# A graph layer on one core: the late nodes' x part of the hidden layer moved from the end of the program to its start

## What is computed

```python
agg = jax.ops.segment_sum(edge_attr, col, num_segments=x.shape[0])
h = jnp.concatenate([x, agg, u[batch]], axis=1)
h = jax.nn.relu(h @ W1 + b1)
out = h @ W2 + b2
return out + x
...
x = _layernorm(x + _L0_gnn_ref(x, edge_index, edge_attr_128, ...), axis=-1)
```

## Time and profile before

| | us |
|---|---|
| median of 3 runs | 185.27 (185.25 to 185.79) |
| the profiled execution | 185.73 |
| its span, first to last instruction | 184.0 |

### The profile page before, as it was taken

One profiled execution on the slowest core, in us unless ns is written; L12 is line 12 of the kernel. 1 busy time (PEld: TensorE's weight loads), 2 busy tenths in 40 slices (PEclk: granted clock), 3 DMA queues, 4 the chain that ended last, 5 costly groups with the idle time before them and its releaser, 6 DMA issues.

```text
span 184.0 us, 5378 instructions
## 1 busy us (share of the span) xinstructions
PE 154.1 (84%) x2195; PEld 113.9 (62%) x2195; DVE 115.4 (63%) x369; ACT 51.5 (28%) x110; POOL 25.4 (14%) x29
## 2 busy tenths in 40 slices
PE   0056979979979979969979999899889799899970
PEld 0046855955955956845846858467458568677850
DVE  6847499568376385485495466954933745877371
ACT  2021233223323313313313343133133241233230
POOL 7800030110200200200200204002003230000000
PEclk9999999999999999999999999999999999999997
DMA  5999999999999999999999999999999999998011
GB/s 119 315 352 373 374 375 373 371 373 374 374 374 373 375 372 373 376 372 373 374 373 374 375 373 374 375 373 360 363 374 374 371 374 370 367 398 303 11 43 33
DMA packets 42196, 62.07 MB, mean 337 GB/s; under 512 B 1975, under 2 KB 39541, under 8 KB 42170
## 3 DMA queue, kind: packets, MB, share of 16 engines
q1 hardware_dynamic: 41046, 61.23, 95.0%
q10 hardware_dynamic: 1124, 0.48, 1.2%
HBM read 58.50 MB, written 3.20 MB: 335 GB/s over the span
## 4 chain that ended last, share of the span: by engine, by line
PE 44%; DMA 39%; SPq 8%; DVE 4%; ACT 1%; issue 1%; DVEq 0%
DMA edge_ring<-in_edge_attr_dram 37%; PE sum_ps L845 17%; PE turn_ps L867 7%; PE hid_ps L907 6%; PE hid_ps L900 6%; PE out_ps L920 5%; SPq L276 4%; SPq L291 3%; DMA base_row<-in_dst_dram 2%; DVE bases L568 2%; PE xt_ps L920 1%; PE xt_ps L882 1%; DVE local_rows L576 1%; ACT local_t L429 1%; PE xt_ps L834 1%
## 5 line engine op out<-in xcount | busy, mean ns | idle before, releaser
L845 PE MATMUL sum_ps<-edge_ring,onehot 128*32 128x128 f32 x1662 | 58.5, 284 | 13.0 <-DMA edge_ring<-in_edge_attr_dram 10.8
L845 PEld LDWEIGHTS sum_ps<-edge_ring,onehot 128*32 128x32 f32 x1662 | 45.2, 113 | 27.9 <-DMA edge_ring<-in_edge_attr_dram 13.3
L630 DVE TENSOR_TENSOR agg_t<-agg_t,turn_ps 128x128 f32 x70 | 20.2, 288 | 56.7 <-PE turn_ps L867 52.6
L594 DVE TENSOR_TENSOR onehot<-iota,local_t 128x768 f32<-128x768 f32 (+1 forms) x40 | 33.6, 843 | 3.0 <-ACT local_t L429 2.4
L402 POOL TENSOR_TENSOR x_all<-x_all,half_b 128x512 f32<-128x512 f32 (+3 forms) x16 | 17.7, 1115 | 127.4 <-PE xt_ps L882 127.4
L466 ACT ACTIVATE hid_t<-hid_ps,bias 128x512 f32<-128x512 f32 (+3 forms) x32 | 18.1, 584 | 37.1 <-PE hid_ps L907 37.1
L867 PE MATMUL turn_ps<-place,sums 128*128 128x128 f32 (+1 forms) x140 | 26.5, 306 | 0.0
L907 PE MATMUL hid_ps<-agg_t,w_a 128*128 128x512 f32 (+3 forms) x64 | 24.1, 500 | 0.6 <-DVE agg_t L630 0.5
L867 PEld LDWEIGHTS turn_ps<-place,sums 128*128 128x128 f32 (+1 forms) x140 | 18.9, 192 | 8.0 <-issue 7.9
L920 PE MATMUL out_ps<-w_sb,hid_t 128*128 128x128 f32 (+1 forms) x176 | 21.9, 275 | 0.0
L441 ACT COPY sums<-sum_ps 128x256 f32<-128x256 f32 (+2 forms) x40 | 13.6, 341 | 25.9 <-PE sum_ps L845 25.9
(11 more groups left out here) (64 smaller groups left out, 73.0 us busy)
## 6 DMA issues: line engine op xcount, KB each, us to landing
edge_ring<-in_edge_attr_dram SPq DMA_DIRECT2D x69, 768.0 KB, 12.1
x_all<-in_x_dram SPq DMA_DIRECT2D x10, 256.0 KB, 10.5
out_dram<-x_all SPq DMA_DIRECT2D x1, 2304.0 KB
dst_rows<-in_dst_dram SPq DMA_DIRECT2D x1, 384.0 KB
x_all<-in_x_dram SPq DMA_DIRECT2D x1, 384.0 KB, 11.1
out_dram<-x_all SPq DMA_DIRECT2D x3, 128.0 KB
out_dram<-x_all SPq DMA_DIRECT2D x1, 256.0 KB
w_x<-in_L_gnn_W_dram ACTq DMA_DIRECT2D x1, 128.0 KB, 5.9
```

The source lines that it names most:

```text
L594: nc.vector.tensor_tensor(onehot[0:ROWS, b % BUFFERS, 0:k * TILES], cols, loc, ALU.is_equal).then_inc(onehot_ready, 1)
L630: nc.vector.tensor_tensor(to, to, turn_ps[b % 2][:, i * SPAN:(i + 1) * SPAN], ALU.add).then_inc(group_added, 1)
L845: last = nc.tensor.matmul(bank[c * WIN:(c + 1) * WIN], onehot[0:p, b % BUFFERS, i * TILES + c * R + r], edge_ring[0:p, slot, c * R + r], s ...
```

## The change

**Start.** The late x is loaded behind the destinations and ahead of group 0, which now stands behind the wait for the pad. `w1_x` is ACT's first load. PE turns the late x in three parts into banks of PSUM that are free at that time, ACT copies them (`copy_x_late`), PE multiplies them by `w1_x` (`sum_x_late`), and ACT keeps the products in SBUF, in `x_hid_late` (`keep_x_hidden`). The first part's product stands ahead of the turning of the destinations, the other two behind it, and PE starts the first batch when all are kept. x of blocks 7, 8 and 9 is loaded two groups earlier than before.

**Late pieces.** `sum_hidden_a` of a late piece starts its own PSUM group. DVE adds the kept product to it into `x_hid_late` (`add_x_hidden`, one add for each half of the hidden layer), and ACT's relu reads from there.

**Order.** The hand-written lists from step 30 on are replaced by loops on `out_step` and `hidden_step`, with `hidden_step` of A set to 31. On DVE `normalize` stands ahead of `step` there, and `add_x_hidden` behind `moments`. ACT takes the root ahead of the copy of the step. The limits for the check of the input's form are made with 15 operations and one reduction in place of 10 and 9.

```diff
@@ -27,6 +27,7 @@
 J = BLOCK // P
 EPS = 1e-5
 GEN_TILES = 10
+COMPLETE_AT = [6, 12, 18, 24, 30, 36, 40, 46, 52, 58, 60, 63, 66, 67, 69]
...
@@ -84,15 +87,25 @@
         return range(batch_first[b], batch_first[b + 1])
 
 
-    hidden_step = [batch_first.index(complete_at[n]) for n in range(n_big)]
+    late_step = batch_first.index(single0)
+    hidden_step = [batch_first.index(complete_at[n]) for n in range(n_pieces)]
+    hidden_step[A] = max(hidden_step[A], late_step + 1)
     out_step = [b + 1 for b in hidden_step]
     turn_x_step = [1] + out_step[:n_big - 1]
-
-
-
-    x_parts = [(n,) for n in range(n_big)] + [(A, B), (C_, D, E), (REST,)]
-    x_load_at = {1: 0} | {IT * n: n for n in range(1, n_big)}
-    x_late_at = 53
...
+
+
+    late_parts = [(A, B), (C_, D, E), (REST,)]
+    n_late = len(late_parts)
+    x_parts = late_parts + [(n,) for n in range(n_big)]
+    x_load_at = {1: 0} | {complete_at[n - 1]: n for n in range(1, n_big)}
+    x_order = [n for part in x_parts for n in part]
+    late_cols = [sum(pieces[n][1] * pieces[n][2] for n in part) for part in late_parts]
+    late_col = [sum(late_cols[:k]) for k in range(n_late)]
...
+        late_turned = [turn_ps[0], turn_ps[1], sum_ps[0]]
+        late_hidden = [[sum_ps[1][:, :], hid_ps[1][:, :]], [turn_ps[0][:, :], turn_ps[1][:, :]],
+                       [sum_ps[0][:, m * late_cols[2]:(m + 1) * late_cols[2]] for m in range(m_chunks)]]
...
-            load_group(0)
+                                 ).then_inc(x_landed[2], 16)
+
 
             sp.wait_ge(pad_set, 1)
-            sp.dma_start(dst_rows[64:full_grp], dst_full[64:full_grp]).then_inc(dst_landed, 16)
-            sp.dma_start(dst_rows[full_grp:n_grp, 0, 0:rest_edges],
+            sp.dma_start(dst_rows[pad0:full_grp], dst_full[pad0:full_grp]).then_inc(dst_landed, 16)
+            sp.dma_start(dst_rows[full_grp:n_grp].rearrange("g c e -> g (c e)")[:, 0:rest_edges],
                          dst[full_grp * EDGES_GRP:n_edges].rearrange("(o e) -> o e", o=1)).then_inc(dst_landed, 16)
-            for g in range(1, n_grp):
+            load_x_late()
+            for g in range(n_grp):
                 load_group(g)
                 if g in x_load_at:
                     load_x(x_load_at[g])
-                if g == x_late_at:
-                    load_x_late()
...
+            act.dma_start(w1_x[:], w1[0:d, :]).then_inc(w1_x_landed, 16)
             act.dma_start(base_row[0:1, 0:n_grp],
                           dst.rearrange("(o e) -> o e", o=1)[:, 0:n_edges:EDGES_GRP],
                           allow_slow_non_contiguous=True).then_inc(bases_landed, 16)
             for to, src in loads:
                 act.dma_start(to, src, allow_slow_non_contiguous=True).then_inc(weights_landed, 16)
+
+            def copy_x_late(k):
+                act.wait_ge(x_turned, k + 1)
+                at = 0
+                for n in late_parts[k]:
+                    _, p, j = pieces[n]
+                    last = nc.scalar.copy(x_t_late[:, late_cols_of(n)].rearrange("f (p j) -> f j p", j=j),
+                                          late_turned[k][:, at:at + p * j].rearrange("f (j p) -> f j p", j=j))
+                    at += p * j
+                last.then_inc(x_t_ready, 1)
+
+            def keep_x_hidden(k):
+                act.wait_ge(late_x_summed, k + 1)
+                for m in range(m_chunks):
+                    last = nc.scalar.copy(x_hid_late[:, m, late_col[k]:late_col[k] + late_cols[k]], late_hidden[k][m])
+                last.then_inc(late_x_ready, 1)
+
+            for k in range(n_late):
+                copy_x_late(k)
+            keep_x_hidden(0)
 
             lt = local_t[:].rearrange("p (g t) -> p t g", t=TILES)
             t0 = 0
@@ -430,6 +482,8 @@
                                       ps[0:ROWS, 0:(t1 - t0) * n_grp].rearrange("p (t g) -> p t g", g=n_grp))
...
+                nc.scalar.copy(x_t[:, n % 2].rearrange("f (p j) -> f j p", j=J),
+                               xt_ps[:, :].rearrange("f (j p) -> f j p", j=J)).then_inc(x_t_ready, 1)
 
             def relu(n):
                 _, p, j = pieces[n]
+                late = n >= n_big
                 for m in range(m_chunks):
-
-                    act.wait_ge(hidden_summed, m_chunks * n + (m + 1 if n < n_big else m_chunks))
+                    if late:
...
+                    else:
+                        act.wait_ge(hidden_summed, m_chunks * n + m + 1)
                     if n >= 2 and m == 0:
 
                         act.wait_ge(out_summed, n - 1)
+                    src = x_hid_late[:, m, late_cols_of(n)] if late else hidden_bank(n, m)
...
                                                        rstd_n[:, jj:jj + 1], ALU.subtract, ALU.mult)
                     last.then_inc(normalized, 1)
 
+            def add_x_hidden(n):
+
+                dve.wait_ge(hidden_summed, m_chunks * (n + 1))
+                if n == A:
+                    dve.wait_ge(late_x_ready, n_late)
+                for m in range(m_chunks):
+                    xh = x_hid_late[:, m, late_cols_of(n)]
+                    nc.vector.tensor_tensor(xh, hidden_bank(n, m), xh, ALU.add).then_inc(late_added, 1)
+
             def moments(n):
...
-            late_step = batch_first.index(single0)
             for b in range(late_step):
                 step(b)
                 if CHECK0 <= b < CHECK0 + 3:
                     check(b - CHECK0)
-                for n in range(n_big):
+                for n in range(LAST):
                     if out_step[n] + 1 == b:
                         moments(n)
                     if out_step[n] + 2 == b:
                         normalize(n)
-            b = late_step
-            step(b)
-            step(b + 1)
-            moments(LAST)
-            step(b + 2)
-            normalize(LAST)
-            step(b + 3)
-            moments(A)
-            step(b + 4)
-            normalize(A)
-            step(b + 5)
-            moments(B)
-            step(b + 6)
-            normalize(B)
-            step(b + 7)
-            step(b + 8)
-            moments(C_)
-            step(b + 9)
-            normalize(C_)
+            for b in range(late_step, n_batch):
+                for n in range(LAST, n_pieces):
+                    if out_step[n] + 2 == b:
+                        normalize(n)
+                step(b)
+                for n in range(LAST, n_pieces):
+                    if out_step[n] + 1 == b:
+                        moments(n)
+                for n in range(A, E):
+                    if hidden_step[n] == b:
+                        add_x_hidden(n)
             add_batch(n_batch - 1)
-            moments(D)
-            normalize(D)
+            add_x_hidden(E)
+            add_x_hidden(REST)
+            for n in range(LAST, E):
+                if out_step[n] + 1 >= n_batch:
+                    moments(n)
+                if out_step[n] + 2 >= n_batch:
+                    normalize(n)
...
+            def turn_x_late(k):
+                pe.wait_ge(x_landed[k], 32 if k == n_late - 1 else 16)
+                if k == 1:
+
+                    pe.wait_ge(x_landed[0], 16)
+                at = 0
+                for n in late_parts[k]:
+                    _, p, j = pieces[n]
+                    for jj in range(j):
+                        last = nc.tensor.transpose(late_turned[k][:, at:at + p], x_all[0:p, x_slot[n] + jj],
+                                                   ident[0:p, 0:p])
+                        at += p
+                last.then_inc(x_turned, 1)
+
+            def sum_x_late(k):
+                pe.wait_ge(x_t_ready, n_late if k == n_late - 1 else k + 1)
+                for m in range(m_chunks):
+                    last = nc.tensor.matmul(late_hidden[k][m], w1_x[:, m * P:(m + 1) * P],
+                                            x_t_late[:, late_col[k]:late_col[k] + late_cols[k]], start=True, stop=True)
+                last.then_inc(late_x_summed, 1)
+
+            pe.wait_ge(consts_ready, 3)
+            for k in range(n_late):
+                turn_x_late(k)
+            pe.wait_ge(w1_x_landed, 16)
+            sum_x_late(0)
+
             pe.wait_ge(consts_ready, 4)
-
             pe.wait_ge(rel_ready, 1)
             nc.tensor.transpose(out_ps[0:C, rel_at], rel[0:n_grp, :], ident[0:n_grp, 0:n_grp]).then_inc(rel_turned, 1)
             pe.wait_ge(rel_t_ready, 1)
...
                 if col == per_bank - 1 or t == TILES - 1:
                     last.then_inc(local_turned, 1)
 
+            pe.wait_ge(x_t_ready, n_late)
+            for k in range(1, n_late):
+                sum_x_late(k)
+
             def sum_group(b, i, g):
...
                 pe.wait_ge(group_added, complete_at[n])
+                if late:
+
+                    pe.wait_ge(hidden_ready, m_chunks * n_big)
+                    if n >= B + 1:
+                        pe.wait_ge(late_added, m_chunks * (n - 1 - n_big))
                 for m in range(m_chunks):
```

(28 more changed lines are left out.)

217 lines of the change are left out of this document (82 added, 135 removed).

## The result

The changed kernel takes 191.49 us (median; 190.77 to 194.48), the kernel before 185.44 beside it: a ratio of 1.031, 95% interval 1.027 to 1.035. The forecast was 188.9 us, 187.2 to 190.8: the direction was right, the loss of 6.1 us is larger than the 3.6 forecast. The profiled execution took 191.8 us, its span 190.0.

What follows compares the result with a forecast made beforehand. Transfers bound the kernel until 144.5 us, then PE; 4.46 us saved on PE was outweighed by VectorE's adds, exposed roots and waits, with 0.3 us for the hole: 3.6 us slower, 188.9 us, range 187.2 to 190.8.

Steps and rivals of the forecast that it cites:

- the hole at the start: Transfers at the start: a gap because group 0 waits for the pad, between nothing and 0.85 us, taken as 0.3.
- the fall of the clock: Rival, chance 0.06: PE idle 3.3 us ahead of C's product drops to 1.2 GHz, 3.5 us doubles, 192.4 us.
- the slower relus: ACT's late relus read SBUF: 0.04 us more each, an estimated 0.3 us for six, left out of the sum.
- signs of being wrong in kind: PE without stalls after 150 us, or the wait for group 59 gone or moved by more than 1 us.
- The sequence on VectorE: Tail: adds, exposed roots and waits cost PE its 4.46 us saving and 2.5 us more by C's product.
- Root waits: Tail: normalization ahead of the step makes DVE wait for ACT's root three times, 2.2 us exposed in all.
- adds: DVE in the tail: two adds per late piece between PE's product and ACT's relu, 0.38 us each at 256 columns.
- PE idle: Tail: PE waits about 1.7 us before A's output, 1.5 before B's product and 3 before C's.
- The product of B: Tail: PE's product for piece B waits for the add of group 62, starting at 161.35 in place of 160.83.
- The lag of PE: Start: first group at about 16.7 in place of 15.40, absorbed by slack at no cost; PE 0.2 us ahead at group 59.
- Each later block gives back more than 1 us: First stretch: PE's spare time waiting for edges, about 1.06 us per block, makes up its late start.
- My faster rival: Whole kernel: PE stays the bound and 4.46 us of its work goes, giving 181.7 us; chance 0.08.

Runs made afterwards that it cites:

- a1: The changed kernel with the normalization on VectorE put back behind the step from step 30 on; 188.98 us.
- a2: The kernel before with only the normalization moved ahead of the step on VectorE; 186.87 us, ratio to before 1.0065.
- b2: The kernel before with only the late x loaded early, behind the destinations, group 0 still first; 185.79 us, ratio to before 1.0007.
- a4: The kernel before with four extra products of 512 columns (3.4 us) on PE once, in step 3; 185.79 us, ratio to before 1.0012.
- c1: The changed kernel with extra matmuls filling PE's waits ahead of the output of A and the products of B and C_; 190.35 us.
- e2: c1 with three more filler matmuls around the last turning and ahead of the products of E and REST; 190.56 us.
- c2: b3 without VectorE's adds and so without the x part of the last 1130 nodes, relus reading PSUM again; 184.61 us.
- d2: c2 with the normalizations one step later and the moments of B behind the next add; 183.32 us.
- b4: The changed kernel with extra matmuls filling only PE's wait ahead of the product of C_; 191.35 us.
- b3: a1 with the load of edge group 0 put back in front of the pad wait; 187.09 us.
- e1: The changed kernel, unchanged, run again beside e2; 191.68 us.
- e3: The changed kernel with only the load of edge group 0 put back in front of the pad wait; 190.29 us.
- b1: The kernel before with only the load of edge group 0 moved behind the pad wait and the destinations; 186.49 us.

## Why the prediction missed by 2.6 us

In short: the step that failed is the hole at the start, priced at 0.3 us and bounded by 0.85, where the edges of group 59 came 1.4 us late. Two terms that the sum held at nothing come on top, the fall of the clock (about 1 us) and the slower relus (0.3 us). One of the forecast's own signs of being wrong in kind came true as well: the wait for group 59 is gone, and the group moved by more than 1 us.

**The sequence on VectorE was right.** Root waits of 0.9, 0.9 and 0.4 were forecast and 0.86, 0.85 and 0.36 came; adds 0.38 and 0.36 (half of 0.72 for the pair); PE idle 1.7, 1.5 and 3 against 1.60, 0.91 and 2.42. The product of B was set for 161.35 and came at 162.64, that of C_ for 170.3 and came at 171.26: both are late by about what group 59 is late, 1.1 us against the forecast's 144.8. (One sum in that part is off by 0.1: 170.3 and 6.49 less 0.45 are 176.3, not 176.2.) a1 and a2 confirm the exposed root by moving it.

**The hole at the start was mis-sized.** I bounded it by nothing and 0.85 us and took 0.3, "since the destinations cover most of it". Group 59 came 1.4 us later than before. The bound itself was wrong: I let the hole end when the pad was ready, at 2.3, but behind that stand two loads of destinations and four of x, and the first long load of edges is issued at 4.85. With it goes a part that missing bytes don't explain, the share of each transfer that falls behind (above). The queue had to be costed to the first edge group, not to the first issue. The late x was fairly priced at nothing (b2).

**The lag of PE: right in cost, wrong in its working.** "Each later block gives back more than 1 us" is false: the wait for edges gave way to waits of 0.7 to 0.8 us for VectorE, so a block gives back some 0.3 us. PE's first group came at 18.5, not 16.7, and the dip of the clock at 30 us, which the forecast did not have, made the lag 5.5 us. a4 lost at most 0.4 us by its interval for a lag of 3.4 us, and b2 nothing that can be told with its dip; in the kernel after the lag took up the whole wait at group 59, which had been forecast to keep 0.2 us, and might have cost something had the edges been in time.

**The clock was a rival at 0.06, and it came true in part.** It stood at 192.4 from an idle time of 3.3 us, with 3.5 us lost. The idle time was 2.42 and did it as well; from the product of C_ to the turning of group 68 PE took 7.76 us (171.26 to 179.02) where I had 5.9, so 1.8 us arose there, and about 1 us shows in medians. My error was to let only the longest wait decide. The longest wait that I quoted as leaving the clock full was 1.1 us; the trace of before had one of 1.68 us with full clock behind it, and I had nothing between that and 3.3:

```profile
80.34 0.86 PE L845 MATMUL sum_ps<-edge_ring,onehot 128*32 128x128 f32 x24 [1.68 <-DMA edge_ring<-in_edge_attr_dram]
```
```profile
80.00:85.00 5.00, 4.66 (x36) 2.48 (x36) 4.62 (x17) 1.21 (x3) 0.00 (x0) 1.00 1.06 373
```

The wait of 2.42 us fell in that gap. The Trainium skill's page "TensorE: Matmul & The Clock Gate", section "What's actually happening", makes activity the condition of the full clock; the fillers of c1 and e2 agree with that.

**The relu from SBUF.** It was left out of the sum. Pairs took 0.94 for 0.84 with 256 columns, so 0.05 us for each, and in c2, where the same pieces are read from PSUM again, they are back at 0.84. That is near the 0.04 us that the forecast had estimated from the figures of the Trainium skill's page "VectorE: DVE Perf Modes", section "The TRN2 errata". Six in the chain are 0.3 us.

**The sum.** By the marks of the table: 1.4 from the start; in the tail 1.9 clock (after to e2), 1.2 the order (e2 to a1), 1.8 the adds less what PE saved (a1 to before), 6.3 in all. Steps from one profile to the next add up to the whole by their making, so this divides the loss and does not prove the parts. The forecast had 0.3 for the start and 3.3 for the tail; 1.4 and 4.9 came. My faster rival, 181.7, was further off than its 0.08 said: c2, without any adds, stays at 184.6.

## What to carry to other kernels

Before work is taken off the engine that looks like the bound, ask what stands second: here VectorE was about 1 us behind PE, so 4.46 us of matmuls were worth 1 us as VectorE's order stood and 2.3 with the order changed as well (d2), and the adds that paid for them 2.5. Price a move in a DMA queue up to the first large load behind it, not up to the first issue. Where a change opens several waits of 1.5 to 2.5 us on PE, as this one did, a fall of its clock belongs in the sum with a chance, not only among the rivals.

## What the runs showed of the hardware that I had not expected

The same wait of 1.60 us on PE was followed by half clock in one kernel (b4, 161 to 166 us) and by full clock in another (after, and also a1, b3, e1 and e3), with the same instructions ahead of it. A wait of 2.07 us, b1's for group 59, was followed by full clock, while those of 2.42 and 2.43 us in after, e1 and e3 all have half clock behind them. So which of several waits brings the fall could not be read off their lengths, and with the waits of the kernel after in place, only filling all of them kept the tail at full clock.

Group 0 standing behind the first small loads cost more than the bytes that were missing at the start: a share of each transfer fell behind in the first 25 us (first to last landing signal of group 6 3.0 to 3.8 us apart, in place of 0.6 to 1.7) and was still behind at the end, so that from 171 to 172 us about 150 GB/s still moved where the other order had finished.
